# An attention and expert block on one core: the fill ahead of the loop written out, and outputs normalised two head groups at a time

## The chip, the cores and the metric

The kernel runs on one core of one Trainium2 chip. The metric is the time of one execution on the device, in microseconds (us). The core's engines are TensorE (PE), VectorE (DVE), ScalarE (ACT), GpSimd (POOL) and SyncE (SP), which issues most DMAs. Each engine works through a program of its own in order, and they wait for one another through semaphores.

## What is computed

One transformer block over x of shape (8, 256, 128): a conditioned layer norm, causal attention with 16 heads of 8 channels, a second norm, and a feed-forward part of 8 experts. Expert 0 has the clean weights and the other seven share one perturbed copy. That copy changes the largest and the smallest 5% of each weight's magnitudes, so the exact order statistics of |W1| and |W2| are needed (`jnp.sort` in the reference).

```
mod = (_silu(L0_c) @ L0_wmod).reshape(L0_c.shape[0], 6, 1, -1)
...
h = _layernorm(x) * (1 + ca) + sa
x = x + ga * attention(h)      # scores/sqrt(8) - slopes*rel, causal, softmax, @ v, @ W_o.T
h = _layernorm(x) * (1 + cb) + sb
x = x + gb * ffn(h)            # router softmax over 8 experts, gelu(h @ W1 + b1) @ W2 + b2
```

## The kernel before

A **step** t is the unit of the main loop: one group of 4 heads of one batch, so 4 steps for a batch and 32 for all. In step t, TensorE builds the scores of group t (`s_unit`, three parts j = 0, 1, 2), VectorE takes their row maxima (`maxima`), and, 5 steps later (E_LAG), TensorE builds the transposed scores (`e_unit`), ScalarE takes their exponential (`exp_unit`, L548), GpSimd masks them (L489), TensorE multiplies by the values (`pv`, L790) and transposes the result into bank psU (`ut`, L807). VectorE then normalises the outputs of that head group: a reciprocal of the row sums (L1355) and a product (L1361) into `A`.

Beside this runs a **bit search** for the order statistics: one round a step, 31 rounds. In a round ScalarE counts with two or three passes over |W1| and |W2| (`sign_count`, L560), VectorE counts with one or two (`dve_counts`, L1136), TensorE adds the counts over the partitions (`total`, L902), and VectorE decides (`decide`, L1142) and writes the next candidates (`next_cand`, L1148). The next round's counts need these. Rounds 0 and 1 come ahead of step 0; from round 2 on ScalarE makes three passes.

Before step 0 comes the **fill**. In the kernel before it is part of the same loop, which starts at t = -10 (T_FIRST) and asks a table of steps what is due: batch 0 and batch 1 are normalised (`ln1`, then n1), transposed (L958), scaled on ScalarE into h1T (L617), projected to queries and keys (L965), split into three bf16 parts (L532 to L538 and L1084 to L1090 for batch 0, L1343 for batch 1) and written to DRAM for re-stacking; the values are projected (L975) and copied by ScalarE into Vx (L640). VectorE also writes rows of the modulation: `gate_sizes` (L1043, L1099), `other_mod_rows` (L1103, L1104) and `gate_signs` (L1108 to L1112).

`spare(k)` puts k matmuls of 512 columns on TensorE whose result nobody reads (L688). The selection's passes read the candidates that VectorE wrote last:

```
act.wait_ge(q["cand_done"], n + 1)
...
pe.wait_ge(q["m_dve"], n + 1)
pe.wait_ge(q["m_act"], signs_through(n))
```

A value copy of batch b waits for its projection, and the transposition of batch b + 1 for that copy:

```
act.wait_ge(q["v_done"], b + 1)
...
pe.wait_ge(q["v_out"], b)
```

## Time and profile before

| | us |
|---|---|
| median of 3 runs | 246.72 |
| their range | 245.69 to 247.44 |
| the profiled execution's own time | 246.49 |
| its span in the profile | 244.8 |
| TensorE busy | 217.0 (89%) |
| VectorE busy | 195.2 (80%) |
| ScalarE busy | 169.4 (69%) |
| GpSimd busy | 143.2 (58%) |

The span runs from the first to the last instruction; the execution's own time has 1.7 us around it. The profile's pages name the line of kernel.py for each group. Four stages follow one another: the fill up to step 0 at 24.1 us, the main loop up to about 186 us, the experts' matmuls up to about 241 us, and the last outputs. A busy share is an average over these stages.

### The profile page before, as it was taken

How to read it: one execution, taken by the hardware profiler on the slowest of the kernel's cores; microseconds unless marked ns; L12 is line 12 of the kernel's file. 1: busy time of each engine (PE TensorE's matmuls, PEld its weight loads, DVE VectorE, ACT ScalarE, POOL GpSimd, SP SyncE). 2: the span in 40 equal slices, each digit the busy share in tenths (PEclk: the TensorE clock that was granted, in tenths of full speed). 3: DMA queues.
4: the chain of work that ended last, by engine and by line, in shares of the span. 5: the costliest groups of instructions: out<-in, count | busy, mean ns of one | idle time of the engine just before them, and what ended most of it. 6: DMA issues, size and time to landing. Idle time of an engine off the chain costs nothing.

```text
span 244.8 us, 5563 instructions
## 1 busy us (share of the span) xinstructions
PE 217.0 (89%) x1848; PEld 143.6 (59%) x1864; DVE 195.2 (80%) x621; ACT 169.4 (69%) x401; POOL 143.2 (58%) x232
## 2 busy tenths in 40 slices
PE   5898888989988989987979879997998999999993
PEld 2454555655655766564656646664554687764783
DVE  2549999999899999999999888884897394764474
ACT  2336767999999988998968967974668552354220
POOL 7652051495887986997585433563859808190710
PEclk9999999999999979999999999999999999999999
DMA  6544673894843722714431500000000001010011
GB/s 198 102 137 143 162 195 98 210 252 130 201 119 98 173 76 83 187 49 122 119 88 60 139 3 5 0 3 3 3 0 1 3 0 44 3 43 0 3 43 44
DMA packets 19155, 20.45 MB, mean 84 GB/s; under 512 B 1367, under 2 KB 17382, under 8 KB 18062
## 3 DMA queue, kind: packets, MB, share of 16 engines
q1 hardware_dynamic: 18438, 19.76, 30.8%
q10 hardware_dynamic: 688, 0.33, 0.5%
q8 instruction: 15, 0.25, 0.5%
q14 instruction: 14, 0.11, 0.2%
HBM read 14.70 MB, written 5.26 MB: 82 GB/s over the span
## 4 chain that ended last, share of the span: by engine, by line
PE 49%; DVE 30%; ACT 11%; issue 8%; DMA 1%; DVEq 0%; ACTq 0%
PE bank L891 12%; PE bank L873 8%; DVE nmax L1165 8%; PE bank L688 4%; DVE msk L1136 4%; ACT msk L560 4%; PE bank L790 3%; DVE nmax L1161 3%; ACT PT L548 3%; DVE cand L1148 2%; PE bank L965 2%; PE bank L856 2%; PE bank L769 2%; PE bank L836 2%; PE bank L747 2%
## 5 line engine op out<-in xcount | busy, mean ns | idle before, releaser
L489 POOL TENSOR_SCALAR_AFFINE_SELECT PT<-PT 128x256 f32<-128x256 f32 (+1 forms) x96 | 45.3, 486 | 38.1 <-ACT PT L548 36.1
L548 ACT ACTIVATE PT<-bank 128x512 f32<-128x512 f32 x96 | 54.8, 608 | 4.2 <-PE bank L764 2.7
L1165 DVE TENSOR_REDUCE nmax<-bank 128x2 f32<-128x512 f32 x64 | 43.3, 681 | 1.9 <-PE bank L747 1.5
L560 ACT ACTIVATE msk<-w2a,cand 128x512 bf16<-128x512 f32 x60 | 43.0, 729 | 0.0
L462 POOL TENSOR_TENSOR ex<-eul,lg 128x32 f32<-128x32 f32 x4 | 21.7, 5436 | 20.2 <-DVE lg L1227 20.2
L560 ACT ACTIVATE msk<-w1a,cand 128x512 bf16<-128x512 f32 x31 | 22.9, 737 | 6.2 <-DVE cand L1148 5.9
L769 PE MATMUL bank<-Qs,Ks 80*128 80x256 bf16 x128 | 24.8, 276 | 0.7 <-ACT PT L548 0.4
L747 PE MATMUL bank<-Ks,Qs 78*128 78x256 bf16 x128 | 24.5, 274 | 0.0
L1136 DVE TENSOR_SCALAR_CACHE_REDUCE msk<-w1a,cand 128x512 bf16<-128x512 f32 x31 | 23.1, 746 | 1.1
L743 PE MATMUL bank<-mask 128*128 128x256 bf16 x64 | 17.8, 279 | 5.5 <-DVE nmax L1165 4.7
L1161 DVE TENSOR_REDUCE nmax<-bank 128x4 f32<-128x512 f32 x32 | 21.6, 675 | 1.1 <-PE bank L740 0.8
L790 PE MATMUL bank<-PT,Vx 128*32 128x256 f32 x256 | 20.4, 391 | 0.6 <-ACT nmT L609 0.6
L688 PE MATMUL bank<-ones_b 128*128 128x512 bf16 x65 | 18.6, 410 | 0.0
L659 ACT ACTIVATE U<-bank 128x256 f32<-128x256 f32 x32 | 12.6, 394 | 7.0 <-PE bank L795 6.7
L591 ACT ACTIVATE hid<-bank,b1p 128x512 f32<-128x512 f32 x16 | 10.3, 680 | 9.6 <-PE bank L873 9.6
L891 PE MATMUL bank<-w2p,hid 128*128 128x128 f32 x128 | 15.3, 277 | 0.0
L873 PE MATMUL bank<-h2T,w1p 128*128 128x512 f32 x32 | 15.1, 599 | 0.0
L891 PEld LDWEIGHTS bank<-w2p,hid 128*128 128x128 f32 x128 | 14.6, 192 | 0.1
L743 PEld LDWEIGHTS bank<-mask 128*128 128x128 bf16 x64 | 7.2, 112 | 12.7 <-DVE nmax L1165 8.4
L902 PEld LDWEIGHTS bank<-acc,ones_f 128*128 128x128 f32 x62 | 9.2, 188 | 8.8 <-issue 7.0
L807 PE MATMUL bank<-ident,U 128*128 128x128 f32 x64 | 13.5, 294 | 1.0 <-ACT U L659 1.0
L902 PE MATMUL bank<-acc,ones_f 128*128 128x4 f32 x62 | 11.1, 250 | 3.5 <-issue 1.9
(200 smaller groups left out, 511.4 us busy)
## 6 DMA issues: line engine op xcount, KB each, us to landing
Qs<-parts SPq DMA_DIRECT2D x7, 576.0 KB
Ks<-parts SPq DMA_DIRECT2D x7, 576.0 KB
parts<-part SPq DMA_DIRECT2D x7, 384.0 KB, 2.8
rows_bc<-rows_out SPq DMA_DIRECT2D x8, 192.0 KB, 7.9
x_all<-in_x SPq DMA_DIRECT2D x8, 128.0 KB, 7.0
parts<-part SPq DMA_DIRECT2D x8, 128.0 KB, 2.9
out<-ob SPq DMA_DIRECT2D x3, 256.0 KB, 2.3
w_sb<-in_w SPq DMA_DIRECT2D x2, 256.0 KB, 5.1
```

What stands on the lines that cost most here:

```text
L489: gp.affine_select(out=v, in_=v, compare_op=ALU.is_ge, fill=0.0, base=0, pattern=[[0, v.shape[1]], [1, P]], channel_multiplier=-1).then_in ...
L548: act.activation(PT[:, e % 2, j], psE[u % 2][:, :], ACT.Exp).then_inc(q["exp_done"], 1)
L560: act.activation(msk[:, col], w[:, :], ACT.Sign, bias=cand[:, col:col + 1].bitcast(F32), scale=-(1.0 - 2.0 ** -24), accum_out=acc[:, col:c ...
L688: mm(psU.rearrange("p (a k) -> p a k", a=HG), ones_b[:, :], ones4, start=True, stop=True)
L747: last = mm(bank[:, i * S:(i + 1) * S], Qs[0:R_S, r, h, P:S], Ks[0:R_S, r, h, :], start=False, stop=True, skip_group_check=True)
L769: last = mm(bank[:, i * S:(i + 1) * S], Ks[0:R_E, r, h, 0:P], Qs[0:R_E, r, h, :], start=True, stop=True, skip_group_check=True)
L790: mm(psO[32 * i:32 * i + 32, 0:S], Vx[:, b % 4, 0, h, :], PT[:, e % 2, 1 + i // 2, (i % 2) * S:(i % 2 + 1) * S], start=True, stop=False, s ...
L873: mm(psF[ch][:, :], wt[:, ch * P:(ch + 1) * P], h2T[:, p % 2], start=True, stop=True).then_inc(q["f1_done"], 1)
L891: last = mm(bank[:, i * P:(i + 1) * P], hid_of(n)[:, ch, i * P:(i + 1) * P], wt[:, ch, :], start=(ch == 0), stop=(ch == NC - 1), skip_grou ...
L1136: last = ve.tensor_scalar(msk[:, col], w[:, :], cand[:, col:col + 1].bitcast(F32), 0.0, op0=ALU.is_lt, op1=ALU.add, accum_out=acc[:, col:c ...
L1161: ve.tensor_reduce(nmax[:, b % 2, 0, HG * g:HG * (g + 1)], bank.rearrange("p (h k) -> p h k", h=HG), axis=AX.X, op=ALU.max, negate=True).t ...
L1165: ve.tensor_reduce(nmax[:, b % 2, 1, h:h + 2], bank.rearrange("p (h k) -> p h k", h=2), axis=AX.X, op=ALU.max, negate=True).then_inc(q["ma ...
```

## The change

**The fill.** The loop now starts at t = 0, and what stood at t = -10 to -1 is written out ahead of it on each engine, in another order. SP loads batch 0 of x ahead of c, and batch 1 ahead of W1 and W2. VectorE normalises batch 0 first, and |W1|, |W2| are made after the parts of batch 0. Rounds 0 and 1 of the search are begun right behind the parts of batch 0, and batch 1 is transposed and projected beside round 0. The value projection of batch 1 moves into step 0, and the router's sums and constants into steps 0 and 1. Seven bodies of the loop have become functions (`scaled`, `high_parts`, `value_copy`, `turned`, `projected`, `values`, `remainder`) with the same content. The semaphore counts in SETS follow the new order.

**The outputs.** psU is now used whole: an even head group is transposed into one half of each block's 256 columns, an odd one into the other. VectorE takes the reciprocal and the product of both groups at once, in the odd group's step. TensorE waits for it only before an even group's transposition.

```diff
+            block_in(0)
             sp.dma_start(c_in[:, :], c).then_inc(q["c_in"], 16)
-            block_in(0)
             sp.dma_start(wmod_sb[:, :], wmod).then_inc(q["wmod_in"], 16)
+            block_in(1)
             sp.dma_start(w1_sb[:, :], w1).then_inc(q["w1_in"], 16)
             sp.dma_start(w2_sb[:, :, :], w2.rearrange("(c p) d -> p c d", p=P)).then_inc(q["w2_in"], 16)
-            block_in(1)
             sp.dma_start(probe.rearrange("p n c -> p (n c)"), probe_c.partition_broadcast(P)).then_inc(q["probe_in"], 16)
             fixed_rows(0)
+            block_in(2)
...
-            rstd(0, NBLK, 1)
+            deviation("ln_stat", (0,), ve1, mv1, rs1, "ln_rstd")
...
-            for t in range(T_FIRST, T_END):
+            rstd(NBLK, 2 * NBLK, 2)
+            normal(1)
+            rstd(2 * NBLK, 3 * NBLK, 3)
+            normal(2)
+            lower_parts(1)
+
+            for t in range(T_END):
...
-            for t in range(T_FIRST, T_END):
+            scaled(0)
+            first_parts()
+            act.wait_ge(q["w1_in"], 16)
+            act.activation(w1a[:, :], w1_sb[:, :], ACT.Abs).then_inc(q["act_set"], 1)
+            value_copy(0)
+            sign_count(0, 2, w1a)
+            scaled(1)
+            sign_count(0, 3, w2a)
+            high_parts(1)
+            sign_count(1, 2, w1a)
+            sign_count(1, 3, w2a)
+
+            for t in range(T_END):
...
-            spare(2)
...
                 pe.wait_ge(q["vec_in"], 16 * 6)
-                tr(psS[1][:, 0:NC + 3], vecs[:, :], ident[0:NC + 3, 0:NC + 3]).then_inc(q["pe_set"], 1)
+                pe.wait_ge(q["dve_set"], SETS["wo"])
+                tr(psO[:, 0:NC + 3], vecs[:, :], ident[0:NC + 3, 0:NC + 3]).then_inc(q["pe_set"], 1)
...
                 pe.wait_ge(q["u_done"], e + 1)
-                if e:
-                    pe.wait_ge(q["a_done"], e)
+                if e % 2 == 0 and e:
+                    pe.wait_ge(q["a_done"], e // 2)
                 for i in range(NBLK):
-                    last = tr(psU[:, i * P:(i + 1) * P], U[:, e % 2, i * P:(i + 1) * P], ident[:, :])
+                    at = S * i + P * (e % 2)
+                    last = tr(psU[:, at:at + P], U[:, e % 2, i * P:(i + 1) * P], ident[:, :])
                 last.then_inc(q["ut_done"], 1)
...
+            turned(0)
+            spare(3)
+            projected(0)
+            spare(4)
+            values(0)
+            mm(psE[1][0:B, 0:512], c_s[:, :], wmod_sb[:, 2 * D:6 * D], start=True, stop=True).then_inc(q["pe_set"], 1)
+            turned(1)
+            spare(2)
+            projected(1)
+            spare(2)
+            total(0)
+            spare(4)
+            vectors()
+            total(1)
+            spare(2)
+
+            for t in range(T_END):
...
-                    pe.wait_ge(q["a_done"], G * (b + 1))
...
+                if t == 0:
+                    values(1)
...
+            ln1(0)
+            v.wait_ge(q["ln_stat"], 1)
+            ve.tensor_scalar(nm1[:, 0:NBLK], mv1[:, 0:NBLK, 0], -1.0, None, op0=ALU.mult).then_inc(q["neg_mean"], 1)
             v.wait_ge(q["act_set"], 1)
...
-            ln1(0)
+            v.wait_ge(q["neg_mean"], 1)
...
+            ln1(1)
...
+            first_split()
+            v.wait_ge(q["w2_in"], 16)
+            then_self(absolute(w2a[:, :], w2_sb.rearrange("p c d -> p (c d)")))
+            first_cand()
+            dve_counts(0)
+            gate_sizes()
+            ln1(2)
+            decide(0)
+            next_cand(0)
+            dve_counts(1)
+            after_next(0)
+            remainder(1)
+            other_mod_rows()
+            gate_signs()
+            decide(1)
+            next_cand(1)
+            dve_counts(2)
+            after_next(1)
+            vector_columns()
+
+            for t in range(T_END):
...
+                if b is not None and g % 2:
                     v.wait_ge(q["ut_done"], e + 1)
-                    ve.reciprocal(rden[:, :, :], psU[:, 0:S].rearrange("p (i h r) -> p i h r", i=NBLK, h=HG)[:, :, :, HD]
-                                  ).then_inc(q["rd_done"], 1)
-                    v.wait_ge(q["rd_done"], e + 1)
-                    if g == 0 and b >= 2:
+                    pu = psU.rearrange("p (i h r) -> p i h r", i=NBLK, h=2 * HG)
+                    ve.reciprocal(rden[:, :, :], pu[:, :, :, HD]).then_inc(q["rd_done"], 1)
+                    v.wait_ge(q["rd_done"], e // 2 + 1)
+                    if g == 1 and b >= 2:
                         v.wait_ge(q["at_done"], b - 1)
-                    pu = psU[:, 0:S].rearrange("p (i h r) -> p i h r", i=NBLK, h=HG)
-                    ve.tensor_tensor(A[:, b % 2, :, HG * HD * g:HG * HD * (g + 1)].rearrange("p i (h d) -> p i h d", h=HG),
-                                     pu[:, :, :, 0:HD], rden[:, :, :].unsqueeze(3).broadcast_to([P, NBLK, HG, HD]),
+                    ve.tensor_tensor(A[:, b % 2, :, HG * HD * (g - 1):HG * HD * (g + 1)].rearrange("p i (h d) -> p i h d", h=2 * HG),
+                                     pu[:, :, :, 0:HD], rden[:, :, :].unsqueeze(3).broadcast_to([P, NBLK, 2 * HG, HD]),
                                      op=ALU.mult).then_inc(q["a_done"], 1)
...
+                if t == ROUTER_STEP + 1:
                     router_constants()
```

**The order on TensorE around step 0.** Names: mask is the causal mask, Ks, Qs the stacked keys and queries, acc the counts (`total`), ones_b against itself a spare. Before, from the total of round 1 on:

```order
L902 MATMUL bank<-acc,ones_f 128x4
L688 MATMUL bank<-ones_b 128x512 x6
L975 MATMUL bank<-wvT,h1T 128x128 x2
L737 MATMUL bank<-mask 128x512
L740 MATMUL bank<-Ks,Qs 128x128 x4
L902 MATMUL bank<-acc,ones_f 128x4
L688 MATMUL bank<-ones_b 128x512 x2
```

In the changed kernel, from the same total on:

```order
L925 MATMUL bank<-acc,ones_f 128x4
L711 MATMUL bank<-ones_b 128x512 x2
L759 MATMUL bank<-mask 128x512
L762 MATMUL bank<-Ks,Qs 128x128 x4
L925 MATMUL bank<-acc,ones_f 128x4
L711 MATMUL bank<-ones_b 128x512 x2
L765 MATMUL bank<-mask 128x2x128
L769 MATMUL bank<-Ks,Qs 128x256 x2
L765 MATMUL bank<-mask 128x2x128
L769 MATMUL bank<-Ks,Qs 128x256 x2
L711 MATMUL bank<-ones_b 128x512 x4
L952 MATMUL bank<-wvT,h1T 128x128 x2
```

The value projection of batch 1 (wvT,h1T) has moved from ahead of step 0 to the end of it, behind round 2's total and the step's spares, and four of six spares between the totals of rounds 1 and 2 are gone.

**The order on ScalarE around step 0.** Rows that read msk,acc are the search's passes; Vx is the value copy of batch 1. In the changed kernel, from round 1 to round 3:

```order
L595 ACTIVATE msk,acc<-w1a,cand 128x512
L595 ACTIVATE msk,acc<-w2a,cand 128x512
L595 ACTIVATE msk,acc<-w1a,cand 128x512
L595 ACTIVATE msk,acc<-w2a,cand 128x512 x2
L560 ACTIVATE Vx<-bank 128x32x8
L595 ACTIVATE msk,acc<-w1a,cand 128x512
```

Before it is the same order (L560 and L640 in place of L595 and L560): the copy stands between the passes of round 2 and round 3 in both.

**The order on VectorE in round 1.** lgT and n hold the modulation's rows. Before, from the counts of round 1 on:

```order
L1136 TENSOR_SCALAR msk,acc<-w1a,cand 128x512
L1136 TENSOR_SCALAR msk,acc<-w2a,cand 128x512
L1152 TENSOR_TENSOR nxt<-cand,probe 128x4
L1343 TENSOR_TENSOR resid<-bank,part 128x512
L1103 TENSOR_SCALAR lgT<-bank 8x128
L1104 COPY lgT<-bank 8x128
L1142 TENSOR_TENSOR cond<-bank,ktab 128x4
L1148 SCALAR_TENSOR_TENSOR cand<-cond,nxt 128x4
```

In the changed kernel:

```order
L1188 TENSOR_SCALAR msk,acc<-w1a,cand 128x512
L1188 TENSOR_SCALAR msk,acc<-w2a,cand 128x512
L1204 TENSOR_TENSOR nxt<-cand,probe 128x4
L1371 TENSOR_TENSOR resid<-bank,part 128x512
L1155 TENSOR_SCALAR lgT<-bank 8x128
L1156 COPY lgT<-bank 8x128
L1160 TENSOR_SCALAR n<-bank 8x256
L1162 TENSOR_SCALAR n<-n 8x256
L1164 TENSOR_TENSOR lgT<-lgT,n 8x256
L1194 TENSOR_TENSOR cond<-bank,ktab 128x4
L1200 SCALAR_TENSOR_TENSOR cand<-cond,nxt 128x4
```

The three instructions of `gate_signs` have come ahead of round 1's decision.

## Rows read from the trace of the kernel before

**Rows 1.** The page's part 4, the chain that ended last, by engine.

```profile
PE 49%; DVE 30%; ACT 11%; issue 8%; DMA 1%; DVEq 0%; ACTq 0%
```

**Rows 2.** Windows: stretch, length; PE, PEld, DVE, ACT, POOL busy; PEclk, DMA, GB/s.

```profile
46.00:66.00 20.00, 18.20 (x200) 11.78 (x201) 18.18 (x57) 19.64 (x53) 14.41 (x28) 1.00 0.81 200
```

**Rows 3.** Waits of ScalarE, 40 to 130 us: in total, times, longest.

```profile
ACT U L659 <- PE bank L795: 2.6, 5, 0.8
...
ACT PT L548 <- PE bank L764: 1.1, 1, 1.1
```

**Rows 4.** Chain in order of time, start of the fill: start, us, what.

```profile
3.06 2.25 PE bank L688 x5
...
7.33 0.85 PE bank L688 x2
8.18 0.46 PE bank L958 x2
...
9.28 2.07 PE bank L965 x4
...
17.92 0.86 PE bank L965 x4
```

**Rows 5.** Timeline of the fill and steps 0, 1: start, us, engine, line, op, tiles.

```profile
1.25 0.42 SPq L264 DMA_DIRECT2D x_all<-in_x  x1
...
10.36 0.39 DVE L1043 TENSOR_SCALAR w2a<-w_sb 128x512 uint32<-128x512 uint32 x1
...
12.72 0.44 DVE L1090 TENSOR_TENSOR part<-resid,part 128x256 bf16<-128x256 f32 x1
...
16.84 0.56 ACT L617 ACTIVATE h1T<-bank,modT 128x256 f32<-128x256 f32 x1 [0.70 <-PE bank L958]
...
17.47 0.16 DVE L1130 COPY cand<-probe 128x4 uint32<-128x4 uint32 x1
...
19.25 0.15 DVE L1124 TENSOR_TENSOR gsum<-bank,br_bc 128x8 f32<-128x8 f32 x1
...
19.32 0.36 PE L902 MATMUL bank<-acc,ones_f 128*128 128x4 f32 x2 [0.20 <-ACT msk L560]
...
23.16 0.72 ACT L560 ACTIVATE msk<-w1a,cand 128x512 bf16<-128x512 f32 x1 [1.30 <-DVE cand L1148]
...
23.47 0.61 PE L975 MATMUL bank<-wvT,h1T 128*128 128x128 f32 x4
...
24.31 0.41 DVE L1108 TENSOR_SCALAR n<-bank 8x256 f32<-8x256 f32 x1
...
25.06 0.41 DVE L1112 TENSOR_TENSOR lgT<-lgT,n 8x256 f32<-8x256 f32 x1
...
25.29 0.36 ACT L640 ACTIVATE Vx<-bank 128x256 f32<-128x256 f32 x1
...
25.49 0.36 PE L902 MATMUL bank<-acc,ones_f 128*128 128x4 f32 x2 [0.97 <-issue]
...
26.37 0.72 ACT L560 ACTIVATE msk<-w1a,cand 128x512 bf16<-128x512 f32 x1 [0.72 <-DVE cand L1148]
...
27.66 0.38 PE L958 MATMUL bank<-ident,n 128*128 128x128 f32 x2
```

**Rows 6.** Windows of TensorE: stretch, length, busy, PEclk, DMA, GB/s.

```profile
89.00:90.00 1.00, 1.00 (x7) 0.50 0.00 0
```

**Rows 7.** Timeline: a step's normalisation, TensorE behind an idle stretch, a wider operation.

```profile
82.10 0.19 DVE L1355 RECIPROCAL rden<-bank 128x8 f32<-128x8 f32 x1
...
82.33 0.22 DVE L1361 TENSOR_TENSOR A<-bank,rden 128x64 f32<-128x64 f32 x1
...
82.47 0.42 DVE L1196 TENSOR_TENSOR h<-n,rows_bc 128x256 f32<-128x256 f32 x1
...
87.09 0.28 PE L743 MATMUL bank<-mask 128*128 128x256 bf16 x1 [1.01 <-DVE nmax L1165]
...
171.25 0.29 DVE L1290 SCALAR_TENSOR_TENSOR b2p_bc<-bank,b2t 128x128 f32<-128x128 f32 x1
```

More of the change, by code:

```diff
@@ L249, in adaln_block @@
         for name, k in (("sil1", 1), ("sil2", 1), ("silu", 1), ("wq", 1), ("wk", 1), ("sa", 1), ("modT", 1), ("wv", 1),
[L250 to L251 removed]
+                        ("wo", 1), ("absg", 1), ("maxg", 1), ("cb", 1), ("cg", 1), ("sgn", 1), ("sgn2", 1), ("rows", 1),
+                        ("cols", 1), ("wrg", 1), ("beta", 1), ("gs", 1), ("all", 1)):
             count += k
@@ L494, in _ @@
                 b = batch_at(t, AT_N1)
-                if b:
+                if b is not None:
                     normal(b)
                 b = batch_at(t, AT_SPLIT)
-                if b is not None and b >= OWN_SPLIT:
+                if b is not None:
                     lower_parts(b)
@@ L902, in total, with turned, projected, values @@
                 mm(psX[:, 0:4], ones_f[:, :], acc[:, :], start=True, stop=True).then_inc(q["tot_done"], 1)
-            for t in range(T_FIRST, T_END):
+            def turned(b):
+                pe.wait_ge(q["n1_done"], b + 1)
+                if b == 0:
+                    pe.wait_ge(q["dve_set"], SETS["silu"])
+                else:
+                    pe.wait_ge(q["v_out"], b)
+                for i in range(NBLK):
+                    last = tr(psQ[:, i * P:(i + 1) * P], n1[:, b % 2, i, :], ident[:, :])
+                last.then_inc(q["t_done"], 1)
+            def projected(b):
+                pe.wait_ge(q["h1_done"], b + 1)
+                for a in range(2):
+                    bank = psS[1][:, 0:S] if a and b == 0 else psQ[:, a * S:(a + 1) * S]
+                    last = mm(bank, wqkT[:, a, :], h1T[:, b % 2], start=True, stop=True)
+                    if a == 0 and b == 0:
+                        last.then_inc(q["q0_done"], 1)
+                last.then_inc(q["qk_done"], 1)
+            def values(b):
+                pe.wait_ge(q["res_done"], b + 1)
+                for i in range(NBLK):
+                    last = mm(psQ[:, i * P:(i + 1) * P], h1T[:, b % 2, i * P:(i + 1) * P], wvT[:, :], start=True, stop=True)
+                last.then_inc(q["v_done"], 1)
+            turned(0)
[14 more added lines that the diff above has]
+            for t in range(T_END):
                 n = sel_bit(t)
@@ L1060, in _ @@
             ds(ve.tensor_tensor(c_s[:, :], psQ[:, 0:B], c_e[:, :], op=ALU.mult))
-            ln1(0)
+            v.wait_ge(q["neg_mean"], 1)
+            v.wait_ge(q["ln_rstd"], 1)
+            for i in range(NBLK):
+                last = ve.tensor_scalar(n1[:, 0, i, :], x_all[:, 0, i, :], nm1[:, i:i + 1], rs1[:, i:i + 1],
+                                        op0=ALU.add, op1=ALU.mult)
+            last.then_inc(q["n1_done"], 1)
             v.wait_ge(q["pe_set"], 2)
```

140 lines of the change are left out of this document (46 added, 94 removed).

## Prediction, before the changed kernel had run

> **What bounds the kernel now.** I read the page's chain first: TensorE has 49% of it and VectorE 30% [rows 1]. The reader should keep the stages apart. TensorE holds the chain in the fill and in the experts' matmuls at the end; neither part of the change touches those last matmuls, so a gain or loss upstream shifts them whole. The windows of the main loop come next: in 46 to 66 us VectorE is busy 18.18 of 20 us and ScalarE 19.64 of 20 [rows 2]. Two engines are nearly full there, coupled once a step by the search. The waits of ScalarE between 40 and 130 us, four rows, come to 6.8 us; the first and the last stand in [rows 3]. So in 90 us a faster VectorE can pull ScalarE forward by at most 6.8 us. Last I read the fill's timeline [rows 5] for the serial chain of the search: candidates, passes on ScalarE, total on TensorE, decision on VectorE, next candidates.
>
> **The fill, up to the first candidates.** TensorE starts on c. SP now issues batch 0 of x ahead of it, and that issue takes 0.42 us [rows 5], so TensorE's first spare comes at 3.06 + 0.42 = 3.48. From there to 7.33 is 4.27 us of spares, weight transposes and modulation [rows 4], all still there: 7.75. Batch 0 is normalised earlier on VectorE and is ready by then, which takes two spares out of its way; its transposition, 0.46, ends at 8.21. Three spares follow, and at 0.85 for two [rows 4] they take 1.28. The projection starts at 9.49, against 9.28. Its parts are finished 12.72 + 0.44 - 9.28 = 3.88 later [rows 4, 5], at 13.37. Then |W2| takes 0.39 [rows 5], and the first candidates (C) are written at about 13.8. Before they were written at 17.47 [rows 5]. This is the gain of the new order: 3.7 us. The reordered loads cost nothing: |W2| was made at 10.36 in the kernel before [rows 5] and is now made after 13.3, so W1 and W2 may land later; batch 1 lands sooner.
>
> **From C to the end of round 2's passes.** Before, round 2's passes began 23.16 - 17.47 = 5.69 behind C [rows 5]. Two things are added. First, in round 0, the total came at 19.32, 1.85 behind C. Now the scaling of batch 1 (0.56) stands between the two passes (0.72 each), and TensorE's projection (0.86 at the full clock) and two spares (0.43) stand ahead of the total [rows 4, 5]. Candidates 0.16 + pass 0.72 + scaling 0.56 + 0.86 + 0.43 = 2.73, so 0.88 is added. Second, the three instructions of the gate signs, 24.31 to 25.06 + 0.41 = 25.47, so 1.16 [rows 5], come ahead of round 1's decision. Round 2's passes start at 13.8 + 5.69 + 0.88 + 1.16 = 21.5 and the total (T) is taken 25.49 - 23.16 = 2.33 later, at 23.9, against 25.49. Of 3.7 us, 1.6 are left.
>
> **The value copy of batch 1.** ScalarE's next instruction behind round 2's passes is that copy, and behind it are queued round 3's passes. Before, the projection was done at 23.47 + 0.61 = 24.1, and the copy ran at 25.29 without waiting; round 3's passes started at 26.37, 0.88 behind T [rows 5]. Now the projection stands at the end of step 0. The same place on TensorE was reached at 27.66 before, 2.17 behind its total [rows 5]; to this come the projection 0.61 and the copy 0.36. Round 3's passes start 3.14 behind T, 2.26 later than they did. 2.26 - 1.63 gives **0.6 us lost** at the start of round 3. From there the order is the old one, and the search is serial, so the 0.6 stays. Its bounds: if TensorE already runs at the full clock in the projection of batch 0, that takes 0.86 instead of 2.07 [rows 4], which gives -0.6; if the first value copy is held behind four spares at the lower clock, another 0.6 us is lost, so +1.2.
>
> The router's constants, 0.15 [rows 5], now stand on VectorE in step 1 ahead of a decision: **+0.15**, or nothing if the total is late there.
>
> **TensorE's clock.** Its last work ahead of T is round 1's total, two spares and the first score part. That total comes at about C + 2.73 + 0.88 + 2 x 0.72 = 18.9, and the work ends about 1.2 us later. TensorE is then idle from about 20.1 to 23.9, 3.8 us; four spares that stood there are gone. In the trace, TensorE stood idle for 1.01 us and went on at 87.09 [rows 7], and the granted clock was 0.50, that is 1.2 GHz, in 89 to 90 [rows 6]; at the start the projection took 2.07 for what takes 0.86 at 17.92 [rows 4]. I expect the idle stretch at 20 us to bring the same. What stands between T and the copy is 2.17 + 0.61 - 0.38 = 2.4 us of matmuls, which at half the clock would take 2.4 more, or nothing more if the clock holds. I take **+1.8**, near the upper end, since the idle stretch is almost four times the one that was followed by a fall.
> The Trainium skill, page "TensorE: Matmul & The Clock Gate", section "Part 1: The HAM clock gate", says that the throttled clock is the default and only activity releases it. By that alone the whole stretch would be slow, and the sum below would be 0.6 higher. The low clock in the start of this trace agrees.
>
> **The paired normalisation.** Before, a step spends 82.47 - 82.10 = 0.37 us of VectorE on it, 0.74 for two. The wide form isn't in this trace. Its nearest row is 128x128 from PSUM at 0.29, against 0.22 for 128x64 [rows 7]. So a pair takes 0.37 + 0.07 + a hundredth or so for the reciprocal = 0.45, and saves 0.29, 4.6 us of VectorE over 16 pairs. No wait is added: TensorE's even transposition waits for what VectorE did the step before, as it did, and the odd one waits for nothing. What the time gets of it lies between 0 (ScalarE full) and 4.6. Eight of the 16 pairs, 2.3 us, fall in the steps in which both engines are nearly full; in the later steps TensorE is on the chain as well. ScalarE's waits in that stretch come in bursts in the steps where VectorE also has the second norm; the gain can be drawn only there, some two thirds of it. I take **-1.5** for the loop.
>
> **Sum.** 0.6 + 0.15 + 1.8 - 1.5 = +1.05 on the profiled execution's 246.49: **247.5 us**. That execution is 0.2 under the median of 246.72.
>
> **Rivals.**
> - *The clock holds.* The idle stretch of 3.8 us stands against it; that TensorE's idle 1.0 us was followed by a fall once and not at other times speaks for it. 247.5 - 1.8 = 245.7.
> - *VectorE's saving counts in full.* For it: VectorE has 30% of the chain, nearly all of it in this loop [rows 1]. Against it: ScalarE's 19.64 of 20. 247.5 + 1.5 - 4.6 = 244.4, and 242.6 if the clock also holds.
> - *The low clock lasts into step 1* (slower). After the copy TensorE has another stretch of 2.17 with a projection of 0.86 ahead of round 4's total, 2.7 us of it matmuls, all of which would double: 247.5 + 2.7 = 250.2. It decides once the low clock outlasts T by more than about 5 us.
> - *The wide form saves nothing*, because the product over both halves of the bank costs twice the narrow one, or because ScalarE is the real bound: 247.5 + 1.5 = 249.0.
>
> **How the numbers follow.** Chances: my forecast 0.40, its own range 246.2 to 249.2 from the fill's and the clock's bounds; the clock holds 0.22; full saving 0.14; into step 1 0.14; nothing saved 0.10. A measurement of this kernel tells about 1%, 2.5 us, from no change, so the borders are 244.2 and 249.2. Faster: half of the full saving and the lower edge of the holding clock, 0.16. Slower: step 1 and what spills over 249.2 of two others, 0.22. The rest, 0.62, is no difference. The range 244.0 to 250.2 leaves out the tails of both ends.
>
> **What would show it.** Right: first candidates near 13.8; round 2's total near 23.9 with TensorE idle some 3 us ahead of it; ScalarE idle for 2 to 4 us ahead of the value copy of batch 1, released by TensorE; a granted clock of 0.5 in part of 20 to 28; 16 reciprocals of 128x16 and 16 products near 0.29; more waits of VectorE and fewer of ScalarE in the loop. Wrong: step 1 well ahead of 27.7 (then the copy doesn't hold the search), or a loop shorter by more than 3 us from step 6 on.

## The result, and the profile after

| | before | changed |
|---|---|---|
| median of the times shown | 246.95 (245.69 to 247.44) | 250.12 (248.80 to 254.65) |
| ratio, 95% interval | 1 | 1.0126 (1.0074 to 1.0177) |
| the profiled execution: own time, span | 246.49, 244.8 | 250.74, 249.0 |
| busy: PE, DVE, ACT | 217.0, 195.2, 169.4 | 215.8, 193.4, 170.0 |

All times in us. The changed kernel is 1.3% slower. A later comparison (e12 below) gave 1.015 (1.006 to 1.024). Executions more than 1.5% above the fastest of their kernel, here the 254.65, are left out of every ratio, but not of the medians. (The median of before has one time more in it than the three shown ahead of the prediction.)

The page's part 2 of the changed kernel, the granted clock in 40 slices of the span (a slice is 6.2 us):

```profile
PEclk9996779999999999999997999999999999999999
```

Slices 4 to 6, 19 to 37 us, ran at a reduced clock, and one more lies at 131 to 137 us. The kernel before shows one fall only, near 90 us, for which [rows 6] has the row.

The page's part 4 of the changed kernel, the chain by engine, against [rows 1]:

```profile
PE 48%; DVE 26%; ACT 15%; issue 8%; DMA 1%; POOL 1%; SPq 0%; ACTq 0%; DVEq 0%
```

VectorE lost four points of the chain and ScalarE gained four. VectorE is also busy for 1.8 us less (195.2 to 193.4), and the time went up all the same. The timeline of the changed kernel shows where: start, us, engine, line, operation, tiles, and in brackets the idle time ahead of it and who ended it. First the projection of batch 0 on TensorE, and the gate signs on VectorE ahead of round 1's decision:

```profile
8.36 1.13 PE L943 MATMUL bank<-h1T,wqkT 128*128 128x256 f32 x4
...
17.98 0.40 DVE L1160 TENSOR_SCALAR n<-bank 8x256 f32<-8x256 f32 x1
18.41 0.28 DVE L1162 TENSOR_SCALAR n<-n 8x256 f32<-8x256 f32 x1
18.42 1.28 POOL L423 TENSOR_TENSOR part<-resid,part 128x512 bf16<-128x512 f32 x1
18.73 1.25 DVE L1164 TENSOR_TENSOR lgT<-lgT,n 8x256 f32<-8x256 f32 x1
19.91 0.14 DVE L1194 TENSOR_TENSOR cond<-bank,ktab 128x4 uint32<-128x4 f32 x1
```

The first candidates are written at 11.75 (17.47 before), so the new order gained 5.7 us up to there in this execution (over all the kernels with this fill they come at 11.75 to 14.21). The decision of round 1 (cond) is at 19.91, against 22.75: 2.8 us of the lead are left. Then step 0 and the start of round 3:

```profile
20.29 0.72 ACT L595 ACTIVATE msk<-w1a,cand 128x512 bf16<-128x512 f32 x1 [3.37 <-DVE cand L1200]
...
22.62 0.56 PE L925 MATMUL bank<-acc,ones_f 128*128 128x4 f32 x2 [4.35 <-ACT msk L595]
...
24.06 0.63 PE L769 MATMUL bank<-Ks,Qs 78*128 78x256 bf16 x2
...
25.12 1.91 PE L711 MATMUL bank<-ones_b 128*128 128x512 bf16 x4
...
26.83 0.82 PE L952 MATMUL bank<-wvT,h1T 128*128 128x128 f32 x4
27.68 0.39 ACT L560 ACTIVATE Vx<-bank 128x256 f32<-128x256 f32 x1 [5.17 <-PE bank L952]
27.96 0.71 ACT L595 ACTIVATE msk<-w1a,cand 128x512 bf16<-128x512 f32 x1
```

TensorE is idle for 4.35 us ahead of round 2's total. ScalarE stands for 5.17 us at the value copy, with round 3's passes behind it. They start at 27.96; before it was 26.37. And the clock, in windows of 1 us (busy times, then the granted clock, the share of the DMA engines, GB/s):

```profile
19.00:20.00 1.00, 0.00 (x0) 0.00 (x0) 1.00 (x2) 0.00 (x0) 0.71 (x1) 1.00 0.75 178
20.00:21.00 1.00, 0.00 (x0) 0.00 (x0) 0.93 (x5) 0.71 (x2) 0.00 (x0) 0.71 0.85 209
...
26.00:27.00 1.00, 1.00 (x4) 0.63 (x3) 0.06 (x1) 0.00 (x0) 0.00 (x0) 0.50 0.63 180
...
29.00:30.00 1.00, 0.43 (x5) 0.21 (x3) 0.54 (x1) 1.00 (x4) 0.00 (x0) 1.00 0.94 246
30.00:31.00 1.00, 0.72 (x4) 0.49 (x5) 0.45 (x3) 0.64 (x3) 0.00 (x0) 0.83 0.78 197
31.00:32.00 1.00, 1.00 (x5) 0.60 (x4) 0.86 (x4) 0.93 (x3) 0.00 (x0) 0.50 0.61 162
```

The clock fell to half (1.2 GHz) while TensorE was idle and came back in the window of 27. It fell again in that of 30 and stayed low up to 34. Round 4's total stands behind that second stretch, and there the difference to before grows by another 1.85.

The times at which a round is decided (start of cond) make a ledger of both kernels. r is the round.

| | first candidates | r1 | r2 | r3 | r4 | r5 | r24 | r30 | end of span |
|---|---|---|---|---|---|---|---|---|---|
| before | 17.47 | 22.75 | 26.00 | 29.20 | 32.98 | 36.54 | 121.79 | 159.63 | 244.8 |
| changed | 11.75 | 19.91 | 23.22 | 30.67 | 36.30 | 39.82 | 124.14 | 163.53 | 249.0 |
| difference | -5.72 | -2.84 | -2.78 | +1.47 | +3.32 | +3.28 | +2.35 | +3.90 | +4.2 |

Of the 4.2 us, 3.3 are there by round 4: between rounds 2 and 4 the difference goes from -2.78 to +3.32. In the loop it shrinks by 0.9 up to round 24 and grows by 1.55 up to round 30, with the fall of the clock at 131 to 137 us in between.

### The profile page after: what moved, and what is told of

Same layout as the page of the kernel before. It is cut to its first block, busy times and chain, and to the rows that moved or that the text cites. A ratio compares the mean times of both kernels' runs of the same rounds, so it can differ in the third digit from the quotient of the medians.

```text
span 249.0 us, 5504 instructions
## 1 busy us (share of the span) xinstructions
PE 215.8 (87%) x1851; PEld 142.2 (57%) x1851; DVE 193.4 (78%) x590; ACT 170.0 (68%) x401; POOL 143.4 (58%) x231
## 4 chain that ended last, share of the span: by engine, by line
PE 48%; DVE 26%; ACT 15%; issue 8%; DMA 1%; POOL 1%; SPq 0%; ACTq 0%; DVEq 0%
PE bank L914 12%; PE bank L896 8%; DVE nmax L1217 7%; ACT msk L595 7%; PE bank L812 4%; DVE msk L1188 4%; PE bank L711 3%; ACT PT L583 3%; DVE nmax L1213 2%; DVE cand L1200 2%; PE bank L769 2%; PE bank L879 2%; PE bank L791 2%; PE bank L943 2%; PE bank L765 2%
## 5 line engine op out<-in xcount | busy, mean ns | idle before, releaser
L493 POOL TENSOR_SCALAR_AFFINE_SELECT PT<-PT 128x256 f32<-128x256 f32 (+1 forms) x96 | 46.1, 496 | 38.4 <-ACT PT L583 36.5
L595 ACT ACTIVATE msk<-w2a,cand 128x512 bf16<-128x512 f32 x60 | 43.1, 730 | 0.0
L595 ACT ACTIVATE msk<-w1a,cand 128x512 bf16<-128x512 f32 x31 | 22.9, 738 | 7.2 <-DVE cand L1200 6.8
L769 PE MATMUL bank<-Ks,Qs 78*128 78x256 bf16 x128 | 25.7, 284 | 0.0
L765 PE MATMUL bank<-mask 128*128 128x256 bf16 x64 | 18.4, 288 | 5.9 <-DVE nmax L1217 4.9
L812 PE MATMUL bank<-PT,Vx 128*32 128x256 f32 x256 | 20.9, 398 | 0.8 <-ACT nmT L656 0.6
L711 PE MATMUL bank<-ones_b 128*128 128x512 bf16 x52 | 17.4, 455 | 0.0
L925 PEld LDWEIGHTS bank<-acc,ones_f 128*128 128x128 f32 x62 | 9.7, 196 | 13.1 <-issue 11.7
L769 PEld LDWEIGHTS bank<-Ks,Qs 78*128 78x128 bf16 x128 | 13.1, 102 | 2.2 <-issue 0.6
```

The source lines that it names most:

```text
L493: gp.affine_select(out=v, in_=v, compare_op=ALU.is_ge, fill=0.0, base=0, pattern=[[0, v.shape[1]], [1, P]], channel_multiplier=-1).then_in ...
L595: act.activation(msk[:, col], w[:, :], ACT.Sign, bias=cand[:, col:col + 1].bitcast(F32), scale=-(1.0 - 2.0 ** -24), accum_out=acc[:, col:c ...
L765: mm(bank.rearrange("p (h k) -> p h k", h=2)[:, :, P:S], mask5[:, HG, :], mask5[:, 0:2, :], start=True, stop=False, skip_group_check=True)
L769: last = mm(bank[:, i * S:(i + 1) * S], Qs[0:R_S, r, h, P:S], Ks[0:R_S, r, h, :], start=False, stop=True, skip_group_check=True)
L812: mm(psO[32 * i:32 * i + 32, 0:S], Vx[:, b % 4, 0, h, :], PT[:, e % 2, 1 + i // 2, (i % 2) * S:(i % 2 + 1) * S], start=True, stop=False, s ...
```

## The experiments

**The ledger of all kernels.** Each row is one profiled execution. "to r5" runs from the first candidates to round 5's decision, which is the rest of the fill and the first steps; "r5 to r30" is the loop; the tail is what follows up to the end of the span. A column for the first candidates stands apart, because it moves by up to 2.5 us between kernels whose programs are the same up to there (see the last section).

| | fill | normalisation | first cand. | to r5 | r5 to r30 | tail | median time | ratio (95%) |
|---|---|---|---|---|---|---|---|---|
| before | old | single | 17.47 | 19.07 | 123.09 | 85.2 | 246.95 | 1 |
| changed | new | pairs | 11.75 | 28.07 | 123.71 | 85.5 | 250.12 | 1.0126 (1.0074 to 1.0177) |
| e1 | new | single | 12.20 | 27.88 | 123.23 | 85.1 | 250.68 | 1.0189 (1.0122 to 1.0256) |
| e2 | old | pairs | 18.17 | 19.07 | 122.96 | 85.5 | 247.93 | 1.0057 (1.0014 to 1.0100) |
| e3 | new, 14 spares | pairs | 13.65 | 24.24 | 123.78 | 85.4 | 248.47 | 1.0072 (1.0026 to 1.0119) |
| e4 | new, values first | pairs | 13.70 | 24.79 | 125.18 | 85.4 | 248.92 | 1.0101 (1.0019 to 1.0182) |
| e5 | e4, signs later | pairs | 13.81 | 24.92 | 123.18 | 85.5 | 247.48 | 0.9971 (0.9919 to 1.0024) |
| e6 | e5, 10 spares | pairs | 13.64 | 20.33 | 124.00 | 85.4 | 244.52 | 0.9913 (0.9872 to 0.9954) |
| e7 | as e6 | single | 14.21 | 20.35 | 126.73 | 85.1 | 244.0 | 0.9887 (0.9826 to 0.9948) |
| e10 | as e6 | single | 13.56 | 20.34 | 122.96 | 85.1 | 243.76 | 0.9905 (0.9872 to 0.9938) |
| e8 | old | pairs, sum first | 17.95 | 19.08 | 122.11 | 85.0 | 246.06 | 0.9978 (0.9934 to 1.0023) |
| e9 | as e6 | pairs, sum first | 11.91 | 20.33 | 122.11 | 84.9 | 240.92 | 0.9806 (0.9759 to 0.9853) |
| e11 | old | pairs | 17.85 | 19.07 | 127.69 | 85.5 | 249.07 | none |
| e12 | new | pairs | 12.37 | 28.00 | 123.44 | 85.5 | 250.94 | 1.015 (1.006 to 1.024) |

Each ratio is against executions of the kernel before in the same comparison (medians 246.2 to 247.0). The profiled executions of e5 (249.12), e7 (248.18) and e11 (251.82) are among the longest of their kernels. The loop column holds falls of the clock too: near 90 us in the kernel before and in e1, at 39 and 53 us in e7, and near 130 us in the changed kernel, e3, e4, e6, e11 and e12. The loops of e2, e5, e8, e9 and e10 have none.

**e1 and e2: the two halves of the change apart.** e1 keeps the new fill and puts the old normalisation back:

```diff
-                if b is not None and g % 2:
+                if b is not None:
                     v.wait_ge(q["ut_done"], e + 1)
-                    pu = psU.rearrange("p (i h r) -> p i h r", i=NBLK, h=2 * HG)
-                    ve.reciprocal(rden[:, :, :], pu[:, :, :, HD]).then_inc(q["rd_done"], 1)
+                    ve.reciprocal(rden[:, :, :], psU[:, 0:S].rearrange("p (i h r) -> p i h r", i=NBLK, h=HG)[:, :, :, HD]
+                                  ).then_inc(q["rd_done"], 1)
...
```

e2 is the reverse: the kernel before with the paired form.

> The new fill with the old normalisation, one head group a step. My theory: all of the loss is the fill's, through the held value copy and TensorE's low clock, 3.3 us at round 4's decision in the changed kernel's trace; the pairs gave back 1.1 us by round 24. So this kernel is 3 to 5 us slower than the kernel before (250 to 251.5), and its decisions of rounds 4 to 24 are 3.3 us later than before, the same at each. Rival, the pairs cost time: this kernel is faster than the changed one, under 249.

> The old fill with the paired normalisation. My theory: 0.8 to 1.5 us faster than before, 245.2 to 245.9, with round 24's decision 1.1 us earlier than before, drawn in the steps of the second norm. Rival, VectorE alone bounds the loop: 3 us or more faster, under 243.7. Rival, the pairs cost time: over 247.5.

e1: 250.68, ratio 1.0189. The fill alone makes the whole loss: 27.88 from the first candidates to round 5, as in the changed kernel. e2: 247.93, ratio 1.0057. The expectation of a gain of about 1 us missed; by the ratio the pairs alone are at best nothing and at worst 1% slower. Not all of that is the pairs': e2's span is 0.9 longer than before, and 0.7 of it lies ahead of the first candidates (18.17 against 17.47), where the two programs are the same. The loop of e2 takes 122.96 with the clock never reduced, and so does that of e10, which has the single form and no fall either. In the loop the pairs as placed change nothing; in the tail they cost 0.3. The form itself is cheap. The groups of lines of e2, on VectorE:

```profile
L1361 DVE TENSOR_TENSOR A<-bank,rden 128x128 f32<-128x128 f32 x16 | 4.7, 291 | 0.5
L1357 DVE RECIPROCAL rden<-bank 128x16 f32<-128x16 f32 x16 | 3.9, 247 | 3.9 <-PE bank L808 3.9
```

The narrow ones stand at 0.19 and 0.22 in [rows 7]. The wide product costs 0.291, where 0.29 was estimated. A pair takes 0.49 of VectorE from its start to the next instruction's (128.19 to 128.68 in the rows shown with e8), where two narrow ones took 0.74. What e2 lost elsewhere is the question of e8.

**e3: TensorE's idle time filled.** The changed kernel with 14 more spares in step 0:

```diff
                 s_unit(t, 0)
+                if t == 0:
+                    spare(14)
```

> The changed kernel with 14 spare matmuls of 512 columns behind the first score part of step 0, about 3 us at 2.4 GHz in the 4.35 us in which TensorE waits for round 2's total. The order of everything else is the changed kernel's. Clock theory: the granted clock stays at 1.00 through 20 to 35 us; the value copy of batch 1 starts 2.8 us behind round 2's total, not 5.1; round 4's decision comes 3 to 3.5 us earlier than in the changed kernel (33 us), and the whole is 3 us faster, 246.5 to 247.5. Rival, the held copy is all of it and the clock costs little: less than 1 us gained, 249.5 or more.

248.47, ratio 1.0072. In its profiled execution the granted clock stays at 1.00 from 20 to 40 us, and "to r5" falls from 28.07 to 24.24. That is the price of the clock in this fill: 3.8 us, some 2.0 of it between the decisions of rounds 2 and 3 (7.45 to 5.41) and 1.7 between those of 3 and 4 (5.63 to 3.96). The whole kernel was expected at 246.5 to 247.5 and missed that by 1 us; the first candidates of the profiled execution came 1.9 later than in the changed kernel's. What remains is 24.24 against the old fill's 19.07. The timeline of e3 shows the next cause. The total of round 2 comes at 24.57, and the copy at:

```profile
20.69 1.26 DVE L1166 TENSOR_TENSOR lgT<-lgT,n 8x256 f32<-8x256 f32 x1
...
27.39 0.38 ACT L560 ACTIVATE Vx<-bank 128x256 f32<-128x256 f32 x1 [2.91 <-PE bank L952]
27.67 0.71 ACT L595 ACTIVATE msk<-w1a,cand 128x512 bf16<-128x512 f32 x1
```

With the full clock the passes of round 3 start 3.10 behind the total, against 0.88 before. In the next step TensorE is idle in e3 as well, for 0.56 ahead of the transposition and 0.85 ahead of round 3's total (0.57 and 0.85 in the changed kernel), and the clock holds:

```profile
29.00:30.00 1.00, 0.15 (x4) 0.06 (x1) 0.69 (x1) 1.00 (x5) 0.00 (x0) 1.00 0.79 188
```

**e4: the values of batch 1 ahead of step 0.**

```diff
             total(1)
             spare(2)
+            values(1)
 
             for t in range(T_END):
...
-                if t == 0:
-                    values(1)
```

> The changed kernel with the value projection of batch 1 back ahead of step 0, so that ScalarE's value copy waits for nothing; no spares added, so TensorE is still idle ahead of round 2's total and its clock still falls. Held-copy theory: round 3's passes start 1 us behind round 2's total, near 23.7 instead of 27.96, but round 3's total stands behind step 0's matmuls at the low clock and comes near 28.3 instead of 30.28; the whole is 2 to 3 us faster than the changed kernel, 247 to 248. Rival, only the clock counts and the copy is hidden: the same as the changed kernel within 0.7 us.

248.92, ratio 1.0101, where 247 to 248 was expected. ScalarE no longer stands at the copy, and round 3's passes start 0.98 behind round 2's total (25.62 against 24.64). But TensorE was still idle ahead of that total, and the clock fell there (23 to 30 us). Timeline of e4:

```profile
24.44 0.36 ACT L560 ACTIVATE Vx<-bank 128x256 f32<-128x256 f32 x1
24.64 0.56 PE L925 MATMUL bank<-acc,ones_f 128*128 128x4 f32 x2 [3.73 <-ACT msk L595]
...
25.62 0.72 ACT L595 ACTIVATE msk<-w1a,cand 128x512 bf16<-128x512 f32 x1 [0.82 <-DVE cand L1199]
...
30.33 0.34 PE L925 MATMUL bank<-acc,ones_f 128*128 128x4 f32 x2
```

Round 3's total is now late by itself: ScalarE ended its passes at 27.8 and the total came at 30.33, behind 5.1 us of matmuls at half speed. Taken away alone, the clock gives 3.8 (28.07 to 24.24) and the copy 3.3 (28.07 to 24.79).

**e5: the gate signs behind round 1's decision, too.**

```diff
             other_mod_rows()
-            gate_signs()
             decide(1)
             next_cand(1)
             dve_counts(2)
             after_next(1)
+            gate_signs()
             vector_columns()
```

> The changed kernel with two calls of the fill put elsewhere: the values of batch 1 ahead of step 0 (as in e4), and VectorE's gate signs behind round 1's decision, the counts of round 2 and the threshold. Theory A (the first rounds' lead is lost to the signs and to the copy that ScalarE holds up): round 1's decision moves up by about 1.2 (the three signs took 0.35, 0.41 and 1.25), round 2's total falls to 21.5 to 23.5, ScalarE starts round 3's passes within 1 us of it, and round 3 is decided at 27 to 28.5 rather than 30.67; what is left of that lead at step 1 is then up to the clock. If TensorE's clock does not fall, the kernel takes 245 to 247; if it falls as in e4, 248. Theory B (only the clock matters): the time stays at e4's 248.9, since VectorE's and ScalarE's orders don't touch TensorE's idle time.

247.48, with times from 243.98 to 249.12; the ratio, 0.9971 (0.9919 to 1.0024), rests on the lower five of the ten. (The first two signs had taken 0.40 and 0.28, not the 0.35 and 0.41 of the expectation.) The times go with the clock: the four executions with a mean granted clock of 0.993 took 243.98 to 246.37, the six with 0.965 to 0.979 took 246.95 to 249.12. Timeline of one of the six, e5's profiled execution:

```profile
22.79 0.56 PE L925 MATMUL bank<-acc,ones_f 128*128 128x4 f32 x2 [1.84 <-issue]
...
24.14 0.72 ACT L595 ACTIVATE msk<-w1a,cand 128x512 bf16<-128x512 f32 x1 [1.18 <-DVE cand L1199]
...
28.95 0.53 PE L925 MATMUL bank<-acc,ones_f 128*128 128x4 f32 x2
```

Round 1 is decided 6.24 behind the first candidates (8.24 in e4) and round 3's passes start early, but the clock is at 0.50 from 23 to 32 us, and round 5 is decided 24.92 behind the candidates, no sooner than in e4. So the signs' move brought nothing there while the clock was low: it is theory A's case of a falling clock, only that nothing of the lead was left. e6 decides.

**e6: all three.** e5 with `spare(10)` behind the first score unit of step 0, where e3 had 14.

> e5 with ten more filler transposes of TensorE in step 0, behind the first score unit, where TensorE otherwise stands idle until round 2's total. Theory A (all three causes together make up the fill's loss): no stretch of a low clock before 60, round 3 decided before 28, round 4 before 31, the whole lead of about 2 to 3 us kept to the end: 244.5 to 246. Theory B (the loss is in TensorE's own added work of the first steps, not in clock and order): 247 to 248.5, with round 4 decided after 33 as before.

244.52, ratio 0.9913 (0.9872 to 0.9954). Round 3 is decided at 26.60 and round 4 at 30.45; no low clock before 60. Theory A holds, with the spares as a necessary part: they alone part e6 from e5, and "to r5" falls from 24.92 to 20.33. Timeline of e6, round 1's decision to round 3's passes:

```profile
19.68 0.14 DVE L1195 TENSOR_TENSOR cond<-bank,ktab 128x4 uint32<-128x4 f32 x1
...
20.42 2.32 PE L711 MATMUL bank<-ones_b 128*128 128x512 bf16 x10
...
21.99 0.41 DVE L1165 TENSOR_TENSOR lgT<-lgT,n 8x256 f32<-8x256 f32 x1
...
22.23 0.36 ACT L560 ACTIVATE Vx<-bank 128x256 f32<-128x256 f32 x1
...
23.77 0.72 ACT L595 ACTIVATE msk<-w1a,cand 128x512 bf16<-128x512 f32 x1 [1.18 <-DVE cand L1201]
```

The spares fill the wait, the third sign takes 0.41 again, and the copy runs without waiting. "to r5" is 20.33. Against the old fill's 19.07 that is 1.3 more, while the candidates come 3.8 to 5.6 earlier: this fill is a gain of 2.6 to 4.3.

**e7 and e10: the mended fill with the old normalisation.** e6 with e1's edit.

> e6 with the normalisation of one head group at a time, as in the kernel before: the candidate for a kernel faster than both. If the pairs lose nothing once the fill is right: the same as e6 within 0.5. If the pairs cost what e2 showed (0.6 per cent, with a longer wait of TensorE for the residual sum): 0.5 to 1.5 us less than e6, 243.5 to 245.5, and no low clock after 90.

> The kernel of e7 again (the fill mended, one group normalised at a time), beside e9 on one chip, since only three undisturbed times stand behind e7's ratio. If the pairs with the sum first are worth their 1 us: 0.988 to 0.992, 0.8 to 1.5 us above e9. If not: the same as e9.

244.0, ratio 0.9887 (0.9826 to 0.9948), and in the second comparison 243.76, ratio 0.9905 (0.9872 to 0.9938). So in this fill too the pairs bring nothing as they stand (e6: 0.9913). e10 was expected 0.8 to 1.5 above e9 and is 2.8 above it. In e7's profiled execution, 248.18, the fill is as in e10 (20.35), but the clock falls at 39 and again at 53 us and the loop takes 126.73. Why they come there is open.

**e8: where the pairs lose.** The kernel before with pairs, and the residual sum moved ahead of them on VectorE:

```diff
+                b = batch_at(t, AT_Y)
+                if b is not None:
+                    v.wait_ge(q["y_done"], b + 1)
+                    ve.tensor_tensor(x_all[:, b], x_all[:, b], psX[:, 0:S].rearrange("p (i d) -> p i d", i=NBLK),
+                                     op=ALU.add).then_inc(q["x2_done"], 1)
                 b, g, e = lagged(t, E_LAG + 1)
                 if b is not None and g % 2:
...
-                b = batch_at(t, AT_Y)
-                if b is not None:
-                    v.wait_ge(q["y_done"], b + 1)
-                    ve.tensor_tensor(x_all[:, b], x_all[:, b], psX[:, 0:S].rearrange("p (i d) -> p i d", i=NBLK),
-                                     op=ALU.add).then_inc(q["x2_done"], 1)
```

> The kernel before with the normalisation of two groups at once (as e2), and on VectorE the residual sum of a batch put ahead of that normalisation in its step. Theory A (e2's loss comes from TensorE's wait for the residual sum, which stands behind the wider operations: 1.33 us idle rather than 0.96): TensorE waits 0.4 to 0.9 for x_all at 129 to 132, the stretch from round 24's total to round 25's falls from 9.8 to 9.5 or less, and the ratio to the kernel before is 0.994 to 1.001. Theory B (the loss of e2 lies elsewhere, in how late U is read or in a fill that began later by chance): the ratio stays at 1.004 to 1.008 with the sum moved.

246.06, ratio 0.9978 (0.9934 to 1.0023). The step in which a pair is normalised is also the step of the residual sum, and TensorE waits for that sum. The timeline of e2 around it:

```profile
128.19 0.24 DVE L1357 RECIPROCAL rden<-bank 128x16 f32<-128x16 f32 x1
128.47 0.29 DVE L1361 TENSOR_TENSOR A<-bank,rden 128x128 f32<-128x128 f32 x1
128.68 0.41 DVE L1367 TENSOR_TENSOR x_all<-x_all,bank 128x256 f32<-128x256 f32 x1
...
129.23 0.34 PE L994 MATMUL bank<-ones_b,hid 128*128 128x1 bf16 x8 [1.33 <-DVE x_all L1367]
```

And of e8:

```profile
127.61 0.41 DVE L1356 TENSOR_TENSOR x_all<-x_all,bank 128x256 f32<-128x256 f32 x1
127.94 0.24 DVE L1362 RECIPROCAL rden<-bank 128x16 f32<-128x16 f32 x1
...
128.16 0.34 PE L994 MATMUL bank<-ones_b,hid 128*128 128x1 bf16 x8 [0.84 <-DVE x_all L1356]
```

In the kernel before the same wait was 0.95. So the pair saves VectorE time in a step in which TensorE does not wait for it, and takes it in the one where TensorE does. With the sum first the loop takes 122.11 (before 123.09, e2 122.96) and the tail 85.0 (85.2, 85.5): the saving arrives, 1.2 us in all against the kernel before, 1.0 against e10. It isn't the one wait shown: from round 5 to 24 e8 is 0.38 shorter than e2, from 24 to 25 by 0.26 and from 25 to 30 by 0.21. e2 also has three waits of 0.19 of the total for x_all (at 74.8, 93.7 and 112.1 us) that e8 hasn't. The ratio's interval holds 1 and overlaps with that of e2, so this rests on the traces. A second cost goes with the same wait. The wait is 1.32 or 1.33 in all eight profiled executions with the sum behind the pair. In six of them (the changed kernel twice, e3, e4, e6 and e11) a low clock follows. Windows of e6, in which TensorE's wait of 1.33 ends at 125.97:

```profile
127.00:128.00 1.00, 1.00 (x12) 0.67 (x10) 0.95 (x4) 0.53 (x2) 0.80 (x1) 1.00 0.00 0
128.00:129.00 1.00, 1.00 (x13) 0.68 (x16) 0.97 (x3) 0.59 (x2) 0.34 (x1) 0.53 0.00 0
129.00:130.00 1.00, 1.00 (x14) 0.46 (x7) 0.96 (x2) 0.47 (x2) 0.30 (x1) 0.50 0.06 16
```

In the six with 0.84 to 0.97 (before, e1, e7, e8, e9, e10) none follows there. e2 and e5 had 1.33 and kept their clock, so their loops read 122.96 and 123.18, where the six read 123.44 to 127.69.

**e11: e2 again.**

> The kernel of e2 again (the old fill, two groups at once, the residual sum behind), on the chip of e9 and e10, to see whether e2's ratio of 1.0057 and e8's 0.9978 stand apart. Theory A (the sum's place): 1.003 to 1.008 again. Theory B (a difference of chips): 0.996 to 1.001, as e8.

It gave no ratio: its six times spread from 243.76 to 251.82, too far for one. In its profiled execution, 251.82, the wait of 1.33 for x_all ends at 128.92, and the clock is at half from 130.3 to 144. Whether e2's 1.0057 and e8's 0.9978 differ by the chip is therefore not settled by it. That the sum's place matters rests on the ledger's loop column and on e9.

**e9: everything that held.** e6 with e8's edit.

> e6 (the fill mended in three places, two groups normalised at once) with VectorE's residual sum ahead of the normalisation, as in e8. If the sum's place is what cost the pairs, and the two gains add: e6's ratio of 0.991 less the 0.8 per cent between e2 and e8, 0.983 to 0.988, 242 to 243.5, and no low clock at 132 to 136. If the sum's place matters only in the old fill, or e8 was luck: 0.990 to 0.993, as e6.

240.92 (240.32 to 242.54), ratio 0.9806 (0.9759 to 0.9853): 2% faster than the kernel before, and more than the 242 to 243.5 that was expected. The page of e9:

```profile
PE 211.9 (89%) x1861; PEld 140.6 (59%) x1861; DVE 191.8 (80%) x590; ACT 169.9 (71%) x401; POOL 144.0 (60%) x231
...
PEclk9999999999999999999999999999999999999999
```

No slice has a low clock. Against e10 on the same chip, whose fill is the same, the span is 2.7 shorter (239.3 and 242.0). The loop and the tail explain 1.05 of it (122.11 against 122.96, 84.9 against 85.1), as in e8 against before. The other 1.65 lies ahead of the first candidates (11.91 against 13.56), where the two programs are the same. That part belongs to the start of the execution and not to the edit, though all six times of e9 are low. Why that is stays open. Without it, e9 would be at some 242.6, or 0.985 of before, by an estimate from these rows.

**e12: the changed kernel again.**

> The changed kernel as it is, in more executions, beside the mended ones. The first comparison gave 1.0126 from three times. If the low clock in rounds 2 to 4 is a constant of this kernel: 1.010 to 1.017 with no time below 247.5. If it comes only in some executions: two groups of times, one near 246.

250.94, ratio 1.015, no time below 248.2. Its ledger repeats the first within 0.3 us in every part but the first candidates. None of the eight times of the two comparisons is under 248.2, so the loss is there in every execution.

## Why the prediction came out as it did

**The verdict.** 247.5 was forecast and 250.12 measured; this is the rival *the low clock lasts into step 1*, whose price was 250.2. It had 14 in 100. Slower by over 1% had 22. So the mechanism was named, and the likeliest case was not the one that came. That the number fell within 0.1 of that rival's price, and just inside the range, is luck. Against the forecast's terms, the first candidates came 2.05 earlier; round 2's total came 0.8 later behind them, round 3's passes 0.4 later behind the total, rounds 3 to 5 lost 1.5 more, and the pairs lost 0.9 where 1.5 was to be gained. Had the candidates come at the forecast 13.8, as they nearly did in e3 to e6, whose program is the same up to there, the time would have been about 252, outside the range (an estimate from the ledger).

**The first candidates.** Forecast 13.8, measured 11.75 (12.2 and 12.4 in e1 and e12, 13.6 to 13.8 in e3 to e6 and e10, 14.2 in e7). The term of the projection, 2.07 from [rows 4], was sized at the slow pace; in this execution it took 1.13, and the unit ahead of it was shorter as well. The bound of -0.6 for this had been given too narrow: it took only the projection and left out everything else that runs before the candidates. On the other side, TensorE's first spare came at 3.91 and not at 3.48.

**Round 2's total.** Forecast 10.1 behind the candidates, measured 22.62 - 11.75 = 10.87. The step that failed is the price of the gate signs: 1.16 for three, read in [rows 5] where nothing ran beside them; measured 19.91 - 17.98 = 1.93. The last took 1.25 and not 0.41, beside a GpSimd operation of 1.28. In e6, with that operation out of the way, it took 0.41. The trace of the kernel before had such a case to read, though not among the signs: `next_cand`, 0.16 at 33.17, took 0.64 beside the same GpSimd operation.

```profile
36.18 1.15 POOL L425 TENSOR_TENSOR part<-resid,part 128x512 bf16<-128x512 f32 x1
...
36.72 0.64 DVE L1148 SCALAR_TENSOR_TENSOR cand<-cond,nxt 128x4 uint32<-128x4 uint32 x1
```

**The value copy.** Forecast: the copy holds round 3's passes until 3.14 behind the total. e3, at the full clock, gives 27.67 - 24.57 = 3.10. This step was right to a few hundredths, and it was the weightiest of the fill. Its net, 0.6, was computed against a lead of 1.6.

**The clock ahead of the total.** Forecast: idle for 3.8 us, and +1.8. Measured: idle for 4.35, a clock of 0.50 from 21 to 27, and 27.96 - 22.62 - 3.10 = 2.24, a little under the full 2.4. (That 2.4 takes off 0.38 for which the prediction names no row; the size came out right all the same.) The page named in the prediction, "TensorE: Matmul & The Clock Gate" of the Trainium skill, would have had the whole stretch slow (+2.4), and in this stretch the trace agrees, with 0.50 in every window from 21 to 27. At the start of the trace of before, where the prediction has it agree too, the projection does take 2.07, but the granted clock reads 1.00.

**The clock in step 1.** This is the step that failed. The forecast had the clock back for good once TensorE was at work again. It did come back at 27, but fell again at 30. In the windows of 28, 29 and 30 TensorE was busy for 0.79, 0.43 and 0.72, since it had nothing to do until round 3's total. From round 3 to round 4 the difference to before grew by 1.85, of which the clock is 1.67 by e3; the rival's price of 2.7 assumed that all matmuls of that stretch were slow. The idle time of step 1 isn't enough by itself: e3 has the same waits there, and a window of 0.15, and no fall. The second fall came in the three executions of this fill (the changed kernel twice, e1) that had the first some 3 us ahead of it; what brings it is not shown. In the whole fill, e3 prices both falls at 3.8 us.

**The router's constants.** Forecast +0.15. They stand at 33.97 and 34.02 on VectorE, ahead of a total at 35.43: nothing, the other bound.

**The pairs.** The step that failed is the translation of busy time into time. A pair took 0.49 (0.45 forecast) and saves 0.25 (0.29 forecast), so the sizes were nearly right. -1.5 was forecast for the loop. Measured: -0.13 in the loop (0.00 against e10, which lacks the fall near 90) and +0.3 in the tail (e2), and with a fall of the clock at 132 us +0.6 and +0.3 (changed kernel). The prediction saw that TensorE's transpositions gain no wait. It did not ask who else waits behind the wide operations on VectorE: the residual sum, and behind it TensorE (0.95 before, 1.33 now). With the sum ahead of the pair, e8 measures -1.0 in the loop and -0.2 in the tail, or -1.2, which is close to the term as forecast. *The wide form saves nothing* came true as a number, but by neither of the reasons given for it.

**The sum, as it came.** From the ledger: first candidates -5.7; to round 5 +9.0; loop +0.6; tail +0.3; in all +4.2. Of the +9.0, 3.8 is the clock (e3) and 3.9 is the copy and the signs (24.24 to 20.33, e3 to e6); the remaining 1.3 is the longer order itself (e6). This split is for one order of taking them away. The three aren't independent: without the spares, e4 and e5 stand at 24.79 and 24.92.

## What to carry to other kernels

- When work is pulled ahead of a loop, list what each engine has left in the place that it came from. TensorE's emptied place cost 3.8 us here, and fourteen matmuls that nobody reads won it back (ten in the mended order). The signs' move brought nothing until that place was filled too (24.79 to 24.92, then 20.33).
- A copy that one engine makes for another stands in its queue. Move the producer and the copy's wait moves with it, onto whatever is queued behind.
- When operations are merged to save time on an engine, the merged one lands in one of two steps. Ask whether somebody waits behind it there, and if so, put what they wait for first.
- A sum of terms can come out right by misses that cancel. Compare it term by term before calling its mechanism confirmed.
